# An LSTM product placed ahead of the next column's sums in a fused graph kernel

## The chip, the cores and the metric

The program runs on one core of one Trainium2 chip. The metric is the device time of one execution in microseconds (us). The kernel before was timed three times: 854.16, 857.33 and 858.17 us, so the median is 857.33 us.

## The reference, cut to what matters

Four graph layers are applied one after the other to x (64 graphs, 128 nodes, 128 features). Layer 0 holds the LSTMs that this case is about; layer 3 needs the eigenvectors of a 128x128 Laplacian made from the adjacency matrix, which depend on nothing else in the chain.

```python
# layer 0: two graph convolutions, then for p = 1..4 an LSTM over windows of p nodes
def step(carry, x_t):
    h, c = carry
    g = x_t @ Wih.T + h @ Whh.T + bias
    i, f, gg, o = jnp.split(g, 4, axis=-1)
    c = jax.nn.sigmoid(f) * c + jax.nn.sigmoid(i) * jnp.tanh(gg)
    h = jax.nn.sigmoid(o) * jnp.tanh(c)
    return ((h, c), None)
...
# layer 3
L_norm = d_inv_sqrt[:, None] * L * d_inv_sqrt[None, :]
_, U = jnp.linalg.eigh(L_norm)
agg = jnp.einsum('mn,bnd->bmd', U.T, features)
```

Layers 1 and 2 are a graph attention and a causal self-attention; the change does not touch them.

## The kernel before, in words

The kernel does two things at once from about 20 to 530 us. One is the reduction of the Laplacian A to tridiagonal form, one column per step, in 126 steps (`STEPS`). It is a serial chain of tiny operations: each needs the one before. The other is layer 0, cut into pieces that stand between the operations of that chain, on the same engines, in an order written out by hand. There is no scheduler: each engine runs its own list in order, and semaphores tie the lists together.

A step i of the column chain runs so (names as in the trace):

- The vector engine (DVE) scales the column to `u` (trace: `VI<-XI,col_root,col_signed`), then makes `y` from the product A times column (`VI<-bank,col_root,col_signed`), and `v`, `p` and `w3` from them.
- The tensor engine (PE) multiplies `p` by V (`bank<-VI`; below called K), while DVE makes `xy`. From both DVE makes the next column (`XI<-xy,bank`) and half of the update of A (`A<-bank,VI,A`, written to A1).
- PE turns `w3` around (line 848), and makes the next column's sums (`bank<-XI`). DVE copies them out (`sa<-bank`, function `column_sums`); GpSimd (POOL) takes a power of them (`col_root<-sa,neg_half`, line 463), which the next `u` waits for.
- DVE finishes the update of A (`A<-bank,col_q,A`), then takes three small values from the sums (`column_signs`). PE multiplies the new A by the column (`bank<-XI,A`; below called the matvec), which the next `y` waits for.

The LSTM work is cut into 72 units (one time step of half a batch of windows), which `timetable` places. A unit has 512 columns, or 336 for p = 3. Its gates are made by PE, a piece at a time: one matmul by `wih` and, where there is a state, one by `whh`; a piece is two passes in the trace. `window(w)` puts pieces in three places per step: behind the matvec of step i (w = 3i), behind K (3i+1), and behind the next step's sums, ahead of its matvec (3i+2). `room` allows three pieces at w = 3i where n is 336, and one or two where it is 512. The scalar engine (ACT) turns each gate into `G` by a sigmoid or a tanh (line 633), in the order input, candidate, forget, output (`gates`).

The four products of a unit are DVE's, and `first_mixer(i, place)` puts them at one of four places of a step: place 0 at its start, place 1 behind the A1 update, place 2 behind `col_q`, directly ahead of `column_sums(i + 1)`, and place 3 at the step's end, behind the A update, `column_signs(i + 1)` and the wait for the finished A. A unit with a state (36 of the 72) has input gate times candidate at place 2 (`T<-G`), forget gate times cell state at place 3 of the same step (`T<-G,C`), their sum at place 0 of the next step (`C<-T`), which ACT takes a tanh of, and the state `H` or `HT` at place 1. The sum waits for a semaphore of the forget product (`l_fc`).

Two of the 36 units fall behind the last column: one in step 125, whose next-column work is missing, and one in step 127, where `tridiagonal(3)`, five small operations on the bounds of the spectrum, stands between places 2 and 3.

Of the kernel before, what the change touches and what calls it, by code (L numbers as in the profile page):

```python
# [304 lines left out]
def build(nc, A_, out_d):  # L305
    with ExitStack() as ctx:
# [91 lines left out]
        def half4(t):  # L398
            return t[:, :].rearrange("p (b d) -> p b d", b=GB)

        def by_window(a, x):

            return a.rearrange("p (g w b) -> p g w b", g=x.gb // GB, b=GB)

        def at_place(x, place):

            return HT[:, ds(x.b0 // GB, x.gb // GB), place:place + (x.nw - 1) * x.p + 1:x.p, :]
# [583 lines left out]
        def _(e):  # L991
# [8 lines left out]
            def rows(b):  # L1000
                return e.bn_stats(out=stat[:, b, :], in_=X[:, b, :])  # L1001
# [14 lines left out]
            def stats_1(n):  # L1016

                o = COLUMNS[n]
                variances(n)
                e.reciprocal(out=var[:, o], in_=var[:, o]).then_inc(stats_in, 1)  # L1020

            def stats_2(n):

                o = COLUMNS[n]
                e.wait_ge(rstd_rt, n)
                net(e.reciprocal(out=dm[:, o], in_=rootv[:, o]))
                net(TT(dm[:, o], dm[:, o], var[:, o], ALU.mult))
                net(TT(dm[:, o], dm[:, o], rootv[:, o], ALU.add))
                net(TS(rstd[:, o], dm[:, o], 0.5, None, ALU.mult))
                STT(nbias[:, o], mean[:, o], -0.5, rstd[:, o], ALU.mult, ALU.mult).then_inc(ln_rdy, 1)  # L1030
# [12 lines left out]
            def masks(part):  # L1043

                if part == 0:
                    net(TS(gmask[:, :], adj[:, :], 0.0, NEG, ALU.is_equal, ALU.mult))
                if part == 1:
                    net(TS(cmask[:, :], upper[:, :], NEG, None, ALU.mult))
                if part == 2:
                    net(TT(sq[:, :], ones[:, :], upper[:, :], ALU.subtract))  # L1050
                if part == 3:
                    net(TT(sq[:, :], sq[:, :], adj[:, :], ALU.mult))
                if part == 4:
                    net(TT(cmask[:, :], cmask[:, :], sq[:, :], ALU.add))
                if part == 5:
                    e.wait_ge(bl_in, 32)
                    net(TT(bias[:, :], bl[:, 0, :], bl[:, 1, :], ALU.add))

            def first_mixer(i, place):

                g = i - GRAPH_AT
                j = i - STATS_AT
                if 0 <= j < 8 and place < 3:
                    e.wait_ge(x_in[j // 2], 16)
                    for b in range(8 * j + (0, 4, 6)[place], 8 * j + (4, 6, 8)[place]):
                        r = rows(b)
                    net(r)
                if place == 3:
                    masks(i - MASKS_AT)
                for n, at in enumerate(FINISH_AT):  # L1070
                    if place == 0 and i == at:
                        stats_1(n + 1)
                    if place == 2 * n and i == at + 1:
                        stats_2(n + 1)
                if place == 0 and 0 <= g - 1 < NG:
                    e.wait_ge(a_s1, g)
                    TT(half4(T[(g - 1) % 2][5]), half4(bank[3]), bias0[:, :].unsqueeze(1).to_broadcast([P, GB, P]), ALU.add).then_inc(a_b0, 1)
                if place == 2 and 0 <= g - 2 < NG:
                    e.wait_ge(a_s3, g - 1)
                    TT(half4(T[g % 2][4]), half4(bank[5]), bias1[:, :].unsqueeze(1).to_broadcast([P, GB, P]), ALU.add).then_inc(a_b1, 1)  # L1080
                if place in (2, 3):
                    for x in PRODUCT_AT.get(i, []):
                        u, h, n = x.index, x.h, x.n
                        if place == (2 if x.s else 3):
                            e.wait_ge(l_act, x.k0 + 2)
                            if u >= 2:
                                e.wait_ge(l_h, u - 1)
                            TT((T[h][2] if x.s else C[h])[:, 0:n], G[h][:, 0, 0:n], G[h][:, 2, 0:n], ALU.mult).then_inc(l_ig, 1)
                        if place == 3 and x.s:
                            e.wait_ge(l_act, x.k0 + 3)  # L1090
                            TT(T[h][4][:, 0:n], G[h][:, 1, 0:n], C[h][:, 0:n], ALU.mult).then_inc(l_fc, 1)
                if i in FINISH_UNIT_AT:
                    x = FINISH_UNIT_AT[i]
                    u, h, n = x.index, x.h, x.n
                    if place == 0 and x.s:
                        e.wait_ge(l_fc, x.c)
                        e.wait_ge(l_ig, u + 1)
                        TT(C[h][:, 0:n], T[h][4][:, 0:n], T[h][2][:, 0:n], ALU.add).then_inc(l_c, 1)
                    if place == 1:
                        e.wait_ge(l_t, u + 1)  # L1100
                        o = by_window(H[h][:, 0:n], x) if x.s < x.p - 1 else at_place(x, x.p - 1)
                        TT(o, by_window(G[h][:, 3, 0:n], x), by_window(T[h][3][:, 0:n], x), ALU.mult).then_inc(l_h, 1)
# [144 lines left out]
            signs_done = column_signs(0)  # L1247
            for i in range(STEPS):
                first_mixer(i, 0)
                xi, gam, live, rest = XI[i % 2], GAM[:, 0, i:i + 1], GAM[:, 1, i:i + 1], slice(i + 1, P)  # L1250
                u, v = VI[:, 0, i + 2:i + 3], VI[:, 0, i + 1:i + 2]
# [21 lines left out]
                if i < STEPS - 1:  # L1273
                    e.wait_ge(ch_e, m)
                    STT(XI[(i + 1) % 2][:, 0:2], xy[:, :, 1], bank[1][:, 5:6], xy[:, :, 0], ALU.mult, ALU.subtract).then_inc(x_ready, 1)
                link.note(STT(A1[:, rest], bank[1][:, 6:P + 5 - i], w3, A[:, rest], ALU.mult, ALU.add))
                first_mixer(i, 1)
                link.note(STT(c("q"), w3, bank[1][:, 4:5], p, ALU.mult, ALU.add))
                a = link.n
                first_mixer(i, 2)  # L1280
                if i + 1 < STEPS:
                    column_sums(i + 1)
# [314 lines left out]
```

## Time and profile before

| quantity | value |
|---|---|
| median of three executions | 857.33 us (854.16 to 858.17) |
| the profiled execution | 854.29 us, of which the span from the first to the last instruction is 852.3 us |
| PE busy | 767.2 us (90%) |
| DVE busy | 707.1 us (83%) |
| ACT busy | 497.1 us (58%) |
| POOL busy | 186.4 us (22%) |
| mean granted PE clock | 0.974 |
| column chain with LSTM units that have a state | about 193 to 517 us |

Busy time counts an instruction from its start to its end. On DVE the next instruction can start before the one ahead of it ends, so starts are what tell the pace. "Idle before" in a row is the engine's own gap and what ended it.

### The profile page before, as it was taken

What the parts mean: (1) busy time and instruction counts of PE and PEld (TensorE: products, weight loads), DVE (VectorE), ACT (ScalarE), POOL (GpSimd) and SP (SyncE); (2) the same over time, 40 slices, a digit from 0 to 9 for tenths busy, and PEclk for the clock granted to TensorE, in tenths of its full rate; (3) what the DMA queues carried; (4) which work ended last, traced back from release to release, by engine and by line L of the source; (5) the groups of instructions that cost most, each with busy time, mean ns of one, the idle gap of its engine ahead of it and who ended that gap; (6) DMA issues with size and microseconds to landing.
All of it is one profiled execution on the core that took longest, in us unless ns stands there. A gap on an engine that the chain in (4) does not pass through costs nothing.

```text
span 852.3 us, 13730 instructions
## 1 busy us (share of the span) xinstructions
PE 767.2 (90%) x3738; PEld 508.8 (60%) x3738; DVE 707.1 (83%) x3445; ACT 497.1 (58%) x1115; POOL 186.4 (22%) x387
## 2 busy tenths in 40 slices
PE   4699989999998999999999998769978879797998
PEld 3578854445554566666545554647756656576765
DVE  6898779999887898888877878999989999788533
ACT  0379966664444444444433434458967868698675
POOL 3111112222121221121212211523113423250000
PEclk9999999999999999999999999879999989899999
DMA  9200000000000000000000000000000000000122
GB/s 273 61 3 1 1 1 1 1 1 0 1 1 1 2 1 0 1 2 2 0 1 0 1 1 0 2 0 1 2 1 2 1 1 2 0 1 1 50 75 75
DMA packets 13970, 12.16 MB, mean 14 GB/s; under 512 B 1091, under 2 KB 10822, under 8 KB 13894
## 3 DMA queue, kind: packets, MB, share of 16 engines
q1 hardware_dynamic: 10992, 8.47, 3.4%
q10 hardware_dynamic: 2902, 2.82, 1.1%
q8 instruction: 30, 0.49, 0.3%
q14 instruction: 46, 0.38, 0.2%
HBM read 7.10 MB, written 4.19 MB: 13 GB/s over the span
## 4 chain that ended last, share of the span: by engine, by line
issue 44%; DVE 22%; PE 18%; POOL 11%; ACT 3%; POOLq 0%; DVEq 0%
PE bank L740 17%; POOL col_root L463 7%; POOL XI L467 3%; DVE tt L993 3%; DVE stat L1001 3%; DVE HT L993 2%; DVE X L994 2%; DVE uu L993 2%; ACT T L691 1%; PE bank L750 1%; DVE sm L1142 1%; ACT T L569 1%; DVE wih L993 1%; DVE T L993 1%; DVE sm L1138 1%
## 5 line engine op out<-in xcount | busy, mean ns | idle before, releaser
L633 ACT ACTIVATE G<-bank,bias 128x512 f32<-128x512 f32 (+1 forms) x252 | 158.6, 634 | 181.3 <-PE bank L740 161.8
L740 PE MATMUL bank<-HT,wih 128*128 128x512 f32 (+1 forms) x504 | 246.0, 576 | 0.4 <-ACT HT L619 0.4
L463 POOL TENSOR_TENSOR col_root<-sa,neg_half 128x1 f32<-128x1 f32 x126 | 69.0, 548 | 409.5 <-DVE sa L995 409.5
L740 PE MATMUL bank<-H,whh 128*128 128x512 f32 (+1 forms) x288 | 137.6, 560 | 1.3 <-DVE H L993 0.8
L573 ACT COPY T<-bank 128x512 f32<-128x512 f32 x138 | 80.5, 586 | 56.0 <-PE bank L740 37.6
L569 ACT ACTIVATE T<-X,nbias,rstd 128x128 f32<-128x128 f32 x256 | 104.4, 483 | 6.6 <-DVE nbias L994 6.6
L740 PEld LDWEIGHTS bank<-HT,wih 128*128 128x128 f32 x504 | 81.0, 193 | 16.8 <-issue 10.2
L740 PEld LDWEIGHTS bank<-VI 128*128 128x128 f32 x254 | 45.0, 196 | 76.5 <-DVE VI L993 56.9
L740 PEld LDWEIGHTS bank<-XI,A 128*128 128x128 f32 x252 | 44.6, 196 | 57.3 <-DVE A L994 48.5
L750 PE MATMUL bank<-ident,T 128*128 128x128 f32 x256 | 39.8, 282 | 32.5 <-ACT T L691 25.2
L994 DVE SCALAR_TENSOR_TENSOR XI<-xy,bank 128x2 f32<-128x2 f32 x125 | 28.2, 225 | 43.4 <-PE bank L740 35.3
L740 PE MATMUL bank<-VI 128*128 128x129 f32 (+63 forms) x254 | 49.2, 275 | 15.6 <-DVE VI L993 15.4
L626 ACT ACTIVATE T<-C 128x512 f32<-128x512 f32 (+1 forms) x72 | 41.5, 576 | 33.7 <-DVE C L993 33.4
L740 PEld LDWEIGHTS bank<-XI 128*128 128x128 f32 x252 | 39.5, 198 | 29.0 <-DVE XI L994 15.4
L1001 DVE BATCH_NORM_STATS2 stat<-X 128x6 f32<-128x128 f32 x256 | 55.0, 277 | 0.2
L740 PEld LDWEIGHTS bank<-H,whh 128*128 128x128 f32 x288 | 46.6, 191 | 13.2 <-issue 6.8
L750 PEld LDWEIGHTS bank<-ident,T 128*128 128x128 f32 x256 | 29.5, 143 | 38.4 <-ACT T L691 29.1
L740 PE MATMUL bank<-XI,A 128*128 128x2 f32 x252 | 40.2, 229 | 9.7 <-DVE A L994 9.7
L995 DVE TENSOR_SCALAR VI<-XI,col_root,col_signed 128x1 f32<-128x1 f32 x126 | 33.7, 268 | 13.3 <-POOL col_root L463 12.8
L484 POOL TENSOR_TENSOR G<-M,d 128x512 f32<-128x512 f32 (+2 forms) x20 | 24.5, 1235 | 90.9 <-DVE HT L993 67.5
L994 DVE SCALAR_TENSOR_TENSOR X<-bank,sm,X 128x128 f32<-128x128 f32 x128 | 35.8, 341 | 9.7 <-PE bank L740 9.5
L993 DVE TENSOR_TENSOR tt<-HT,G 128x64 f32<-128x64 f32 (+1 forms) x128 | 39.5, 309 | 3.8
(357 smaller groups left out, 1657.2 us busy)
## 6 DMA issues: line engine op xcount, KB each, us to landing
out_x<-T SPq DMA_DIRECT2D x16, 256.0 KB, 2.2
wih<-in_WihT ACTq DMA_DIRECT2D x1, 1024.0 KB, 12.0
whh<-in_WhhT ACTq DMA_DIRECT2D x1, 1024.0 KB, 17.8
qkvT<-in_WqkvT ACTq DMA_DIRECT2D x1, 192.0 KB
wg<-in_Wg ACTq DMA_DIRECT2D x2, 64.0 KB
l3w<-in_L3W ACTq DMA_DIRECT2D x2, 64.0 KB
adjT<-in_adjT ACTq DMA_DIRECT2D x1, 64.0 KB
adj<-in_adj SPq DMA_DIRECT2D x1, 64.0 KB, 2.0
```

The costliest lines, as they stand in the source:

```text
L463: e.tensor_tensor(out=col["root"][:, :], in0=sa[:, 0:1], in1=neg_half[:, :], op=ALU.pow).then_inc(root_ready, 1)
L467: e.tensor_copy(out=XI[(i + 1) % 2][:, 2:3], in_=ident[:, ds(i + 2, 1)]).then_inc(oh_ready, 1)
L569: i = e.activation(T[g % 2][0][:, ds(b % GB * D, D)], X[:, b, :], ACT.Relu, bias=nbias[:, b:b + 1], scale=rstd[:, b:b + 1])
L573: e.copy(out=dst[:, :], in_=src[:, :]).then_inc(done, 1)
L626: e.activation(T[x.h][3][:, 0:x.n], C[x.h][:, 0:x.n], ACT.Tanh).then_inc(l_t, 1)
L633: e.activation(G[x.h][:, gate, 0:n], gate_bank(k)[:, 0:n], ACT.Tanh if gate == 2 else ACT.Sigmoid, bias=bias[:, 4 * (x.p - 1) + gate:4 * ( ...
L740: mm = lambda out, l, r, start=True, stop=True: e.matmul(out, l, r, start=start, stop=stop)
L750: i = e.transpose(dst[:, ds(b * P, P)], src[:, ds(b * P, P)], ident[:, :])
L993: TT = lambda o, a, b, op: e.tensor_tensor(out=o, in0=a, in1=b, op=op)
L994: STT = lambda o, a, s, b, o0, o1: e.scalar_tensor_tensor(out=o, in0=a, scalar=s, in1=b, op0=o0, op1=o1)
L995: TS = lambda o, a, s1, s2, o0, o1=None: e.tensor_scalar(o, a, s1, s2, o0, *([o1] if o1 else []))
L1001: return e.bn_stats(out=stat[:, b, :], in_=X[:, b, :])
```

## The change: forget gate times cell state moves from place 3 to place 2

```diff
                             TT((T[h][2] if x.s else C[h])[:, 0:n], G[h][:, 0, 0:n], G[h][:, 2, 0:n], ALU.mult).then_inc(l_ig, 1)
-                        if place == 3 and x.s:
+                        if place == 2 and x.s:
                             e.wait_ge(l_act, x.k0 + 3)
                             TT(T[h][4][:, 0:n], G[h][:, 1, 0:n], C[h][:, 0:n], ALU.mult).then_inc(l_fc, 1)
```

No instruction is added or removed, and the lists of PE, ACT, POOL and SyncE are the same in both kernels. DVE's list in step 77, which is one of the 336-wide units' (T12 is the product of input gate and candidate, T14 that of forget gate and cell state):

```order
 L993 TENSOR_TENSOR T12<-G1 128x336
+L993 TENSOR_TENSOR T14<-G1,C1 128x336
 L995 TENSOR_SCALAR sa<-bank0 128x3
 L994 SCALAR_TENSOR_TENSOR A<-bank7,col_q,A1 128x50
@@ -1461,5 +1462,4 @@
 L1242 TENSOR_SCALAR col_size<-sa 128x1
 L995 TENSOR_SCALAR GAM<-sa 128x1
-L993 TENSOR_TENSOR T14<-G1,C1 128x336
 L993 TENSOR_TENSOR C1<-T14,T12 128x336
 L995 TENSOR_SCALAR VI<-XI0,col_root,col_signed 128x1
```

The product now stands ahead of the sums' copy and of the A update, and the sum of the two products follows the small values directly. 34 steps of the column chain have this form, 16 of them 336 wide and 18 of them 512 wide. In step 127, behind the last column, DVE's list changes so (`col_lo` to `col_sgm` are `tridiagonal(3)`):

```order
 L993 TENSOR_TENSOR T12<-G1 128x512
+L993 TENSOR_TENSOR T14<-G1,C1 128x512
 L994 SCALAR_TENSOR_TENSOR col_lo<-col_mxe,col_mnd 128x1
 L994 SCALAR_TENSOR_TENSOR col_w<-col_mxe,col_mxd 128x1
@@ -2346,5 +2347,4 @@
 L995 TENSOR_SCALAR col_w<-col_w 128x1
 L1220 TENSOR_SCALAR col_sgm<-col_w 128x1
-L993 TENSOR_TENSOR T14<-G1,C1 128x512
 L993 TENSOR_TENSOR C1<-T14,T12 128x512
```

Here the five small operations come behind the product and its wait for the forget gate.

## Rows read from the trace of the kernel before

**Rows 1.** Groups of PE weight loads, 290 to 405 us: busy, mean ns | idle before

```profile
L740 PEld LDWEIGHTS bank<-XI,A 128*128 128x128 f32 x62 | 9.5, 188 | 13.4 <-DVE A L994 12.8
```

**Rows 2.** Timeline, DVE in step 77 (336 wide): start us, us, operation

```profile
332.72 0.50 DVE L993 TENSOR_TENSOR T<-G 128x336 f32<-128x336 f32 x1
333.14 0.15 DVE L995 TENSOR_SCALAR sa<-bank 128x3 f32<-128x3 f32 x1
333.21 0.26 DVE L994 SCALAR_TENSOR_TENSOR A<-bank,col_q,A 128x50 f32<-128x50 f32 x1
...
333.57 0.49 DVE L993 TENSOR_TENSOR T<-G,C 128x336 f32<-128x336 f32 x1
334.10 0.51 DVE L993 TENSOR_TENSOR C<-T 128x336 f32<-128x336 f32 x1
334.52 0.27 DVE L995 TENSOR_SCALAR VI<-XI,col_root,col_signed 128x1 f32<-128x1 f32 x1
...
335.91 0.22 DVE L994 SCALAR_TENSOR_TENSOR XI<-xy,bank 128x2 f32<-128x2 f32 x1
```

**Rows 3.** Timeline, PE in the same stretch

```profile
333.52 0.38 PE L740 MATMUL bank<-XI,A 128*128 128x2 f32 x2 [0.19 <-DVE A L994]
333.76 0.81 PE L740 MATMUL bank<-H,whh 128*128 128x336 f32 x2
...
334.98 0.73 PE L740 MATMUL bank<-H,whh 128*128 128x336 f32 x2
335.54 0.32 PE L740 MATMUL bank<-VI 128*128 128x51 f32 x2
```

**Rows 4.** Timeline, A update and matvec of step 76 (336 wide)

```profile
329.13 0.26 DVE L994 SCALAR_TENSOR_TENSOR A<-bank,col_q,A 128x51 f32<-128x51 f32 x1
...
329.52 0.32 PE L740 MATMUL bank<-XI,A 128*128 128x2 f32 x2
```

**Rows 5.** Timeline, step 78: sums' copy, and the next u behind POOL

```profile
336.78 0.15 DVE L995 TENSOR_SCALAR sa<-bank 128x3 f32<-128x3 f32 x1
...
337.70 0.27 DVE L995 TENSOR_SCALAR VI<-XI,col_root,col_signed 128x1 f32<-128x1 f32 x1 [0.35 <-POOL col_root L463]
```

**Rows 6.** Timeline, step 100 (512 wide, two pieces behind the matvec)

```profile
419.45 0.25 DVE L994 SCALAR_TENSOR_TENSOR A<-bank,col_q,A 128x27 f32<-128x27 f32 x1
...
420.13 0.28 PE L740 MATMUL bank<-XI,A 128*128 128x2 f32 x2
...
422.07 0.30 PE L740 MATMUL bank<-VI 128*128 128x28 f32 x2
...
422.51 0.23 DVE L994 SCALAR_TENSOR_TENSOR XI<-xy,bank 128x2 f32<-128x2 f32 x1
```

**Rows 7.** Timeline, step 109 (512 wide, one piece behind the matvec)

```profile
454.84 0.69 ACT L633 ACTIVATE G<-bank,bias 128x512 f32<-128x512 f32 x1 [1.25 <-PE bank L740]
...
455.40 0.69 DVE L993 TENSOR_TENSOR T<-G 128x512 f32<-128x512 f32 x1
...
455.83 0.28 PE L740 MATMUL bank<-XI 128*128 128x3 f32 x2
...
456.15 0.16 DVE L995 TENSOR_SCALAR sa<-bank 128x3 f32<-128x3 f32 x1
...
456.92 0.28 PE L740 MATMUL bank<-XI,A 128*128 128x2 f32 x2
...
457.89 0.27 DVE L995 TENSOR_SCALAR VI<-XI,col_root,col_signed 128x1 f32<-128x1 f32 x1
...
458.66 0.40 PE L740 MATMUL bank<-VI 128*128 128x19 f32 x2 [0.50 <-DVE VI L993]
```

**Rows 8.** Timeline, step 127, behind the last column

```profile
526.06 0.15 DVE L994 SCALAR_TENSOR_TENSOR col_lo<-col_mxe,col_mnd 128x1 f32<-128x1 f32 x1
...
526.82 0.15 DVE L1220 TENSOR_SCALAR col_sgm<-col_w 128x1 uint32<-128x1 uint32 x1
527.18 0.69 DVE L993 TENSOR_TENSOR T<-G,C 128x512 f32<-128x512 f32 x1 [0.21 <-ACT G L633]
```

**Rows 9.** Windows: us, busy (count) of PE, PEld, DVE, ACT, POOL; PE clock, DMA share, GB/s

```profile
263.70:267.10 3.40, 1.85 (x8) 1.24 (x9) 3.22 (x16) 0.63 (x1) 0.23 (x2) 1.00 0.00 0
267.10:270.50 3.40, 3.40 (x6) 1.46 (x6) 1.62 (x12) 1.21 (x2) 0.64 (x2) 0.50 0.00 0
```

## The prediction, written before the result was known

> **What bounds the kernel now.** I read the timeline of the column steps first, DVE's rows beside PE's, then the groups of idle time on PE's weight loads, and last the windows with the granted clock. The reader is to see that two engines take turns in bounding a step. In a step with a forget product DVE runs without a gap from the candidate product to the next `u` [rows 2]. At the same time PE waits: the matvec of step 77 starts at 333.52 us, 0.31 behind the start of the A update at 333.21, with the weight load's wait for A ended by it [rows 2, 3]. Over the 336-wide stretch this wait sums to 12.8 us [rows 1]. Behind the matvec stand three LSTM pieces, and directly behind the last of them K: its second half starts one pass (0.28 us, half of the 0.57 between the starts of the last piece and K, 334.98 to 335.54) ahead of K, so K starts the moment PE is free [rows 3]. The next column XI starts at 335.91, which is 0.37 behind K's start [rows 2, 3]; it also stands 1.39 behind `u` (334.52), which is DVE's own shortest way. Both roads arrive together. So the A update is not a side road here: A, matvec, three pieces, K, XI is a chain without slack, and the old place of the product, behind the A update, kept that chain short.
>
> **What the change moves, part by part.** Nothing is added; 36 products move. Two are behind the last column, 34 in the chain, in three kinds by what PE has behind the matvec. I counted them in the timetable's windows and PE's timeline.
>
> *What the product costs in its new place.* The 336-wide product T<-G at 332.72 holds the next instruction until 333.14, so 0.42 us; the 512-wide one holds it 0.60 where nothing is waited for (in step 109 `sa` comes 0.75 behind it, since it waits for the sums that PE started at 455.83, 0.32 earlier [rows 7]; the 0.60 is the 0.69 of the row less the overlap of 0.08 that the 336 one shows, 0.50 against 0.42 [rows 2, 7]). `sa`, the A update and everything behind them come later by that.
>
> *What it gives in its old place.* From the old product's start to the sum's start is 0.53 in step 77 (333.57 to 334.10), because the sum waits for the product's end. That falls out, so DVE reaches `u` 0.53 - 0.42 = 0.11 earlier. But the next `u` also waits for POOL's power: in step 78 it starts 0.92 behind `sa` [rows 5]. In step 77 `sa` moves to 333.56, the power lets `u` go at 334.48, against 334.52 before. The gain is 0.04.
>
> *Kind 1, 16 steps, 336 wide (three pieces behind the matvec; in the last, two of 512).* Eight are like step 77: A waits 0.42 longer, the matvec starts at 333.94, three pieces and K follow in the same 2.02 us (333.52 to 335.54), K starts at 335.96 and XI at 336.33: 0.42 later, 0.40 by finer reading over the eight. Eight are like step 76: there the matvec at 329.52 is 0.39 behind A's start at 329.13 and not 0.31, since PE came from an earlier piece, so 0.08 is slack and 0.34 passes [rows 4]; over the eight I read 0.33. One step (69) has 0.2 of slack at K. Sum: 8 x 0.40 + 8 x 0.33 - 0.2 = 5.6 us lost.
>
> *Kind 2, 8 steps, 512 wide, two pieces (once three of 336) behind.* In step 100 the A update at 419.45 would let the matvec go at about 419.76 (0.31 behind it), but it starts at 420.13, since a 512-wide piece is ahead of it on PE. Of the 0.60, 0.37 is slack, and 0.23 reaches K at 422.07. XI at 422.51 is 0.44 behind K and needs 0.34 to 0.37, so another 0.1 is slack, and 0.13 passes [rows 6]. The others lie between 0.09 and 0.18; together 1.1 us. PE is then later by 0.1 to 0.2 than DVE, and in about half of these steps the next `sa` sits on PE's sums: 0.6 more. Sum 1.7 us lost.
>
> *Kind 3, 10 steps, 512 wide, one piece or none behind.* In step 109 `sa` waits for PE's sums until 456.15, and the product fills that wait: the new `sa` comes at 455.40 + 1.20 = 456.60, 0.45 later and not 0.60. The way from there to `u` loses the old product with its wait (0.72). So `u` comes 0.27 earlier. K had waited 0.50 for DVE, which covers the later matvec, so the 0.27 is kept [rows 7]. Six to seven steps are like this, three have 0.18. Sum 2.5 us gained.
>
> *The two behind the last column.* In step 125 the product fills a short wait of the A update: 0.1 gained. In step 127 the product starts at 527.18 when the forget gate comes, and the five small operations from 526.06 to 526.97 that had used the wait now stand behind it [rows 8]: up to 0.9 lost, of which later waits for PE may swallow a third. I take 0.6; net 0.5 lost.
>
> *The added wait.* The forget gate must be there earlier. Its latest arrival in the chain is step 109, ACT's row from 454.84 to 455.53, while the product would start at 456.00 [rows 7]. It costs nothing; if ACT were 0.5 later, `sa` and all behind it on DVE would wait.
>
> Sum: 5.6 + 1.7 - 2.5 + 0.5 = 5.3 us lost. The profiled execution took 854.29 us (span 852.3, so 2.0 around it); this gives 859.6. That execution was 3.0 under the median of 857.33; from the median the sum gives 862.6. I take the middle, 861.0.
>
> **A rule weighed against the rows.** Rows 2 show the next DVE instruction starting 0.08 us ahead of the end of a 336-wide product. The Trainium skill, "VectorE: DVE Perf Modes", section "The DRAIN you can't avoid", says that the next op does not start until the pipe is empty, and that leaving out a semaphore wait between two ops saves nothing. It speaks against this change: nothing of kind 3's gain from the dropped wait would be left, and the A update would be later by the whole duration. The row disagrees with it by 0.08 per product, so I keep it as a rival only.
>
> **The rivals.**
>
> *DVE alone counts (faster).* If the matvec had slack after all, for example if K could go ahead of the pieces, each step would be worth its change of `u`: 16 x 0.06 + 8 x 0.13 + 10 x 0.25 = 4.5 us gained, 852.8 us from the median. For it: DVE shows no gap in rows 2. Against: K starts as PE's last pass ends [rows 3]. It decides if the matvec's delay is under the slack at K, which is 0 in kind 1.
>
> *Products hold DVE for their whole duration (slower, more).* 0.50 instead of 0.42 in 16 steps adds 1.3, 0.69 instead of 0.60 adds 0.7 in kind 2 and takes 0.9 from kind 3: 8.2 us lost, 865.5 us.
>
> *The granted clock falls once or twice more.* In this trace the clock was at half (1.2 GHz) from 267.1 to 270.5, behind a stretch of 3.4 us in which PE was busy for only 1.85; PE was then busy for all 3.40, so a fall costs about 1.7 us [rows 9]. The change adds 0.3 to 0.4 us of idle PE in front of many matvecs. Two more falls: 5.3 + 3.4 = 8.7 lost, 866.0 us. Against: single gaps stay under 1 us, and the pieces fill the rest.
>
> *The lateness is made good.* If pieces behind a late matvec ran closer together, or the neighbouring step's slack took most of kind 1's delay, the losses of kinds 1 and 2 would halve to 3.7, and with kind 3 and the end the sum is 1.7 lost: 859.0 us. For it: step 69's slack. Against: steps 71 to 73, 76 to 78 and so on follow one another with K at the 1.02 behind `u` of rows 2 and 3 (334.52 to 335.54), which is the tight value.
>
> **How the numbers follow.** 0.5% is 4.3 us, about what a measurement of this kernel can tell from no change. Forecast 0.66 (its 5.3 is near that bound: 0.40 above, 0.26 under); DVE alone 0.12 (0.09 faster, 0.03 same); whole durations 0.07, slower; clock 0.08 (0.07 slower, 0.01 same); made good 0.07 (0.06 same, 0.01 faster). Faster 0.10, same 0.36, slower 0.54. The forecast's own range is 858 to 864; with the rivals I leave out most of "DVE alone" below 855 and little above 866.5.
>
> **What would show it.** Kind 1: the weight load of `XI,A` waits about 0.4 longer per step (the 12.8 us become about 18), XI waits for K by 0.4 more in the steps behind them, and steps 76 to 78 grow. Kind 3: steps like 109 shrink by about 0.27 us. The wait of `C<-T` goes. Wrong if the matvec wait grows and XI does not move, or if the forget gate shows up as what DVE waits for inside the chain.

## The result, and the profile after

The changed kernel takes 861.46 us in the median of 15 executions (856.99 to 863.15); the kernel before, executed 15 times beside it and earlier, 855.15 us (851.37 to 858.17). The ratio is 1.0063, with a 95% interval of 1.0048 to 1.0078, which is 5.4 us lost (4.1 to 6.7). Forecast were 861.0 us and 5.3 us lost. The time of 861.0 was taken halfway between two sums from three executions; with the median of all 15 the forecast loss gives 860.5.

| quantity, profiled execution | before | after |
|---|---|---|
| span | 852.3 us | 858.7 us |
| mean granted PE clock | 0.974 | 0.972 |
| DVE busy | 707.1 us | 703.4 us |
| idle before XI, all steps, behind PE | 35.3 us | 47.6 us |
| idle before the matvec's weight load, behind A, all steps | 48.5 us | 63.3 us |

One thing differs from what was said ahead of the prediction. DVE's list is shorter by one semaphore wait per moved product: the trace of the kernel before has 766 such records on DVE, that of the change 730. They took no time of their own (between the last of the small values and the next product it is 0.06 us with and without one), but they shift the numbering of DVE's instructions, which matters further down.

The groups of PE's weight loads in the same 31 steps as in [rows 1] (now 290 to 412 us; busy, mean ns | idle before):

```profile
L740 PEld LDWEIGHTS bank<-XI,A 128*128 128x128 f32 x62 | 9.5, 188 | 19.4 <-DVE A L994 18.8
```

The wait for A has grown from 12.8 to 18.8 us. The timeline of step 77, DVE, answers to [rows 2]:

```profile
334.58 0.50 DVE L993 TENSOR_TENSOR T<-G 128x336 f32<-128x336 f32 x1
335.00 0.50 DVE L993 TENSOR_TENSOR T<-G,C 128x336 f32<-128x336 f32 x1
335.42 0.15 DVE L995 TENSOR_SCALAR sa<-bank 128x3 f32<-128x3 f32 x1
335.49 0.26 DVE L994 SCALAR_TENSOR_TENSOR A<-bank,col_q,A 128x50 f32<-128x50 f32 x1
...
335.85 0.50 DVE L993 TENSOR_TENSOR C<-T 128x336 f32<-128x336 f32 x1
336.31 0.27 DVE L995 TENSOR_SCALAR VI<-XI,col_root,col_signed 128x1 f32<-128x1 f32 x1
...
338.18 0.23 DVE L994 SCALAR_TENSOR_TENSOR XI<-xy,bank 128x2 f32<-128x2 f32 x1 [0.59 <-PE bank L740]
```

and PE in the same step to [rows 3]:

```profile
335.80 0.38 PE L740 MATMUL bank<-XI,A 128*128 128x2 f32 x2 [0.60 <-DVE A L994]
336.05 0.81 PE L740 MATMUL bank<-H,whh 128*128 128x336 f32 x2
...
337.82 0.32 PE L740 MATMUL bank<-VI 128*128 128x51 f32 x2
```

From T<-G to the matvec it was 0.80 us (332.72 to 333.52) and is 1.22 (334.58 to 335.80). From the matvec to K it is 2.02 as before, and XI is 0.36 behind K. XI now waits 0.59 for PE, 1.87 behind `u` and not 1.39, though DVE reached `u` 0.07 sooner behind T<-G (1.73 against 1.80).

The time from one XI to the next, step by step, after less before, shows where the whole change lies. The sums over the kinds, in us (kinds 1 to 3 are those of the prediction):

| kind | steps | forecast | measured |
|---|---|---|---|
| 1: 336 wide | 16 | +5.6 | +5.5 |
| 2: 512 wide, two or three pieces behind the matvec | 8 | +1.7 with the steps behind them | +1.9, and +0.6 in the steps behind them (step 117 left out) |
| 3: 512 wide, one piece or none | 10 | -2.5 | -2.4 |
| behind the last column: XI of step 124 to the table M | 2 | +0.5 | +0.8 (19.05 to 19.82) |

The rows add up to 6.4 us here, near the upper end of what the timing gives. The span has grown by 6.4 too, but by chance: outside the rows of the table gains and losses cancel. Steps 5 and 6 are 1.3 us shorter (DVE waits less for PE there), step 22 is 1.5 shorter (a clock fall that is missing), steps 60 and 61 are 1.6 longer, and there are short gaps of DVE of both signs, of which the next section tells. Step 117 is left out of the steps behind kind 2, since it is 0.28 shorter by such a gap in the profile before. Steps 60 and 61 have a longer clock fall, at the place of [rows 9] (columns as there):

```profile
260.90:264.30 3.40, 1.78 (x9) 1.10 (x9) 3.23 (x13) 0.63 (x1) 0.61 (x2) 0.99 0.00 0
264.30:271.10 6.80, 6.67 (x12) 3.37 (x12) 2.42 (x18) 1.89 (x3) 0.69 (x2) 0.50 0.00 0
```

It lasts 6.8 us and not 3.4, behind the same two steps without pieces on PE. But a fall that the kernel before had at 120.4 us is missing here. And two of the experiments below, "mixed" and "mixed, both products of kind 1 behind A", have the same lists up to step 68, and one shows this fall with 3.4 us (from 265.3), the other with 6.8 (from 260.9). So its length belongs to the single execution. Over all executions the clock is the same: the mean is 0.973 in the 15 of the change, and 0.972 to 0.974 in the kernel before on the four chips of the experiments.

### The profile page after: what moved, and what is told of

Read it like the earlier page. It is cut to its first block, busy times and chain, and to the rows that moved or that the text cites. A ratio compares the mean times of both kernels' runs of the same rounds, so it can differ in the third digit from the quotient of the medians.

```text
span 858.7 us, 13687 instructions
## 1 busy us (share of the span) xinstructions
PE 770.0 (90%) x3731; PEld 507.4 (59%) x3738; DVE 703.4 (82%) x3445; ACT 500.0 (58%) x1115; POOL 185.8 (22%) x387
## 3 DMA queue, kind: packets, MB, share of 16 engines
HBM read 7.10 MB, written 4.19 MB: 13 GB/s over the span
## 4 chain that ended last, share of the span: by engine, by line
issue 45%; DVE 22%; PE 18%; POOL 11%; ACT 3%; POOLq 0%; DVEq 0%
PE bank L740 17%; POOL col_root L463 7%; POOL XI L467 3%; DVE tt L993 3%; DVE stat L1001 3%; DVE HT L993 2%; DVE X L994 2%; DVE uu L993 2%; ACT T L691 1%; PE bank L750 1%; DVE sm L1142 1%; DVE wih L993 1%; DVE T L993 1%; ACT T L569 1%; DVE sm L1138 0%
## 5 line engine op out<-in xcount | busy, mean ns | idle before, releaser
L740 PEld LDWEIGHTS bank<-XI,A 128*128 128x128 f32 x252 | 42.9, 195 | 69.9 <-DVE A L994 63.3
L994 DVE SCALAR_TENSOR_TENSOR XI<-xy,bank 128x2 f32<-128x2 f32 x125 | 28.1, 225 | 53.2 <-PE bank L740 47.6
L740 PE MATMUL bank<-XI,A 128*128 128x2 f32 x252 | 42.5, 238 | 14.7 <-DVE A L994 12.0
```

The source lines that it names most:

```text
L740: mm = lambda out, l, r, start=True, stop=True: e.matmul(out, l, r, start=start, stop=stop)
L994: STT = lambda o, a, s, b, o0, o1: e.scalar_tensor_tensor(out=o, in0=a, scalar=s, in1=b, op0=o0, op1=o1)
```

## The experiments

All keep PE's, ACT's and POOL's lists and move DVE's products only, unless it is said otherwise. The product's place is chosen by the unit's kind (1 to 3 as above, 4 behind the last column):

```diff
-                        if place == 3 and x.s:
-                            e.wait_ge(l_act, x.k0 + 3)
-                            TT(T[h][4][:, 0:n], G[h][:, 1, 0:n], C[h][:, 0:n], ALU.mult).then_inc(l_fc, 1)
+                        if x.s and place == FC_AT[kind(x)]:
+                            forget(x)
```

With `{1: 3, 2: 3, 3: 3, 4: 3}` it is the kernel before, with four times 2 the change. The line numbers of the kernels below differ from those before by the added lines. Two more places are used: "sums", behind `column_sums(i + 1)`, and "A", behind the A update and ahead of `column_signs(i + 1)`. Per kernel: the median, the ratio to the kernel before on the same chip with its 95% interval, and the sums of XI-to-XI changes by kind in its profile, in us:

| kernel | median us | ratio (interval) | kind 1 | kind 2 | kind 3 |
|---|---|---|---|---|---|
| the change | 861.46 | 1.0063 (1.0048 to 1.0078) | +5.5 | +1.9 | -2.4 |
| kind 1 alone | 860.4 | 1.0044 (1.0026 to 1.0061) | +5.6 | +0.1 | -0.2 |
| kind 2 alone | 856.43 | 1.0004 (0.9988 to 1.0021) | -0.6 | +1.9 | -0.2 |
| kind 3 alone | 852.05 | 0.9960 (0.9941 to 0.9979) | -0.4 | +0.5 | -2.7 |
| kind 4 alone | 858.16 | 1.0015 (0.9997 to 1.0033) | 0.0 | 0.0 | 0.0 |
| kind 1 behind the sums | 859.49 | 1.0047 (1.0026 to 1.0068) | +5.6 | +0.1 | -0.2 |
| kinds 1 to 3 behind A | 851.36 | 0.9955 (0.9935 to 0.9974) | -0.5 | -0.9 | -1.1 |
| mixed | 852.0 | 0.9972 (0.9951 to 0.9993) | -0.5 | -0.9 | -2.4 |
| one piece left out, old order | 854.4 | 0.9990 (0.9974 to 1.0007) | 0.0 | 0.0 | 0.0 |
| one piece left out, kind 1 moved | 854.01 | 0.9989 (0.9975 to 1.0003) | 0.0 | +0.1 | -0.2 |
| mixed, both products of kind 1 behind A | 854.17 | 0.9977 (0.9960 to 0.9994) | +1.5 | -0.9 | -2.4 |

Where a kernel changed nothing in a kind, its sum still comes out between -0.6 and +0.5. This is not noise of the single execution. DVE has short gaps with no wait to explain them; three rows show one:

```profile
382.53 0.27 DVE L995 TENSOR_SCALAR VI<-XI,col_root,col_signed 128x1 f32<-128x1 f32 x1 [0.27 <-issue]
382.90 0.27 DVE L1008 TENSOR_SCALAR VI<-XI,col_root,col_signed 128x1 f32<-128x1 f32 x1 [0.27 <-issue]
379.85 0.27 DVE L1012 TENSOR_SCALAR VI<-XI,col_root,col_signed 128x1 f32<-128x1 f32 x1 [0.27 <-issue]
```

They are step 90 in the kernel before, in kind 4 alone and in one piece left out in the old order. These three have the same DVE list up to step 124, and the same seven gaps, in steps 47, 69, 80, 90, 95, 112 and 117, of 0.15 to 0.37 us. Over all twelve profiles, from 190 to 517 us, 59 instructions that waited for no other engine start over 0.1 us later behind the one ahead of them than the same pair does at its closest. With DVE's records (semaphore waits included) numbered from 0, 56 of the 59 have a number that leaves 63 when divided by 128, and the other three leave 64. So the gaps go by the place in DVE's list. An order that drops semaphore waits shifts all later instructions against them: the change has gaps in steps 75, 80, 107 and 119 instead. What happens at every 128th record no run here shows.

For a sum this means: each kernel carries its own pattern of gaps, each worth up to 0.35 us. Kind 1 in the change comes out 0.8 us low by it, since the kernel before had gaps in steps 69, 80 and 95 that cost it time (0.19, 0.25 and 0.35) and the change has none there that costs any. Half a us is the size of this effect in the other sums.

**Kind 1 alone.** `FC_AT = {1: 2, 2: 3, 3: 3, 4: 3}`

> Only the 16 products of the 336-wide units stand at place 2 (three pieces behind the matvec); the other 20 stay at place 3. Theory (the A update, the matvec, the three pieces, K and XI are a chain without slack, so each product ahead of the A update passes on what it is longer than the matvec's slack): 5.6 us slower than before, about +0.65%, and the matvec's weight load waits about 6 us more in that stretch. Rival (DVE alone counts): 1 us faster. Rival (the lateness is made good by half): 2.8 us slower, +0.33%.

Its 16 products cost 5.6 us in the profile and 3.8 us (2.2 to 5.2) in the timing. The matvec's weight loads wait for A as in the change:

```profile
L753 PEld LDWEIGHTS bank<-XI,A 128*128 128x128 f32 x62 | 9.5, 188 | 19.2 <-DVE A L1007 18.6
```

Six us more wait, and a time well away from "faster". The timing's interval holds the lower rival's 2.8 and ends just short of the theory's 5.6; the steps decide between them: thirteen of the sixteen are longer by 0.36 to 0.42 us each, and the other three (69, 80, 95) are those in which the kernel before has a gap.

**Kind 2 alone.** `{1: 3, 2: 2, 3: 3, 4: 3}`

> Only the 8 products of 512-wide units with two pieces (once three) behind the matvec stand at place 2. Theory: 1.7 to 2.0 us slower, +0.2%. Rival (DVE alone counts): 1.0 us faster, -0.1%.

+1.9 in the steps themselves (each of the eight longer by 0.18 to 0.28), but a timing from -1.0 to +1.8 us does not tell it from nothing. The profile is against the rival, the timing cannot decide.

**Kind 3 alone.** `{1: 3, 2: 3, 3: 2, 4: 3}`

> Only the 10 products of 512-wide units with at most one piece behind the matvec stand at place 2. Theory: the product fills DVE's wait for the next column's sums and the dropped wait of the sum of products is won too: 2.4 us faster, -0.3%. Rival (a product holds DVE for its whole duration, nothing won from the dropped wait): 0.9 us less, 1.5 us faster. Rival (any product ahead of the A update delays): slower.

2.7 us gained by steps, 3.4 (1.8 to 5.1) in the timing. Step 109, DVE, against [rows 7]:

```profile
455.07 0.68 DVE L1006 TENSOR_TENSOR T<-G 128x512 f32<-128x512 f32 x1
455.67 0.68 DVE L1006 TENSOR_TENSOR T<-G,C 128x512 f32<-128x512 f32 x1
456.27 0.15 DVE L1008 TENSOR_SCALAR sa<-bank 128x3 f32<-128x3 f32 x1
...
456.67 0.68 DVE L1006 TENSOR_TENSOR C<-T 128x512 f32<-128x512 f32 x1
```

Each product holds DVE for 0.60 and not for its 0.68, and the sum follows the small values with no wait. A product ahead of the A update is therefore not bad by itself.

**Kind 4 alone.** `{1: 3, 2: 3, 3: 3, 4: 2}`

> Only the two products behind the last column (steps 125 and 127) stand at place 2. Theory: 0.5 to 0.8 us slower, within the noise of the timing; in the profile the way from XI of step 124 to the table M grows from 19.0 us to about 19.8. Rival (later waits for PE swallow it): no change of that way.

The way from XI of step 124 to M is 19.60 us against 19.05. DVE in step 127, against [rows 8]:

```profile
527.29 0.69 DVE L1006 TENSOR_TENSOR T<-G,C 128x512 f32<-128x512 f32 x1 [0.97 <-ACT G L646]
527.90 0.15 DVE L1007 SCALAR_TENSOR_TENSOR col_lo<-col_mxe,col_mnd 128x1 f32<-128x1 f32 x1
...
528.85 0.69 DVE L1006 TENSOR_TENSOR C<-T 128x512 f32<-128x512 f32 x1
```

DVE's wait for the forget gate is 0.97 where it was 0.21, with the five small operations behind it. Up to there step 125 had gained 0.22, and step 127 loses 0.77. The cost is seen in the profile; the timing's interval reaches no change.

**Kind 1 behind the sums.** `{1: "sums", 2: 3, 3: 3, 4: 3}`

> The 16 products of the 336-wide units stand between the copy of the sums (sa) and the A update; all others stay at place 3. So POOL's power starts on time, but the A update is as late as in the change. Theory (the A update's lateness is what costs): 5 to 6 us slower, as with all 16 at place 2. Rival (the late sums and the power behind them cost): no slower than before, 1 to 2 us faster.

DVE, POOL and PE in step 77:

```profile
331.86 0.50 DVE L1006 TENSOR_TENSOR T<-G 128x336 f32<-128x336 f32 x1
332.28 0.15 DVE L1008 TENSOR_SCALAR sa<-bank 128x3 f32<-128x3 f32 x1
332.35 0.49 DVE L1006 TENSOR_TENSOR T<-G,C 128x336 f32<-128x336 f32 x1
332.52 0.74 POOL L476 TENSOR_TENSOR col_root<-sa,neg_half 128x1 f32<-128x1 f32 x1 [3.32 <-DVE sa L1008]
332.77 0.26 DVE L1007 SCALAR_TENSOR_TENSOR A<-bank,col_q,A 128x50 f32<-128x50 f32 x1
...
333.08 0.38 PE L753 MATMUL bank<-XI,A 128*128 128x2 f32 x2 [0.60 <-DVE A L1007]
```

`sa` is on time, 0.42 behind T<-G as before, and A and the matvec are as late as in the change. The cost is the same: +5.6 by steps, ratio 1.0047 against 1.0044. So the late sums and the power behind them are not the cause in kind 1; the late A update is.

**Kinds 1 to 3 behind the A update.** `{1: "A", 2: "A", 3: "A", 4: 3}`

> All 34 products of the column chain stand directly behind the A update, ahead of the three small values; the two behind the last column stay at place 3. Sums and A update are on time, and the small values cover the wait of the sum of products for the forget product. Theory: u comes 0.1 us earlier in each; in the 16 336-wide steps K has no slack, so nothing is won there; in the 18 others it is: 2 us faster, -0.25%. Rival (DVE alone counts): 34 x 0.11 = 3.7 us faster, -0.4%. Rival (a product holds DVE for its whole duration): no change.

Step 77:

```profile
332.37 0.26 DVE L1007 SCALAR_TENSOR_TENSOR A<-bank,col_q,A 128x50 f32<-128x50 f32 x1
...
332.55 0.50 DVE L1006 TENSOR_TENSOR T<-G,C 128x336 f32<-128x336 f32 x1
332.68 0.38 PE L753 MATMUL bank<-XI,A 128*128 128x2 f32 x2 [0.18 <-DVE A L1007]
...
333.56 0.27 DVE L1008 TENSOR_SCALAR VI<-XI,col_root,col_signed 128x1 f32<-128x1 f32 x1
...
335.06 0.22 DVE L1007 SCALAR_TENSOR_TENSOR XI<-xy,bank 128x2 f32<-128x2 f32 x1 [0.21 <-PE bank L753]
```

`u` comes 0.12 sooner behind the A update (1.19 against 1.31), and XI then waits 0.21 for PE: where K is tight the gain turns into that wait. In kind 3 the 0.12 is kept (step 109: 4.31 to 4.19 us from XI to XI). In kind 2 it is kept up to step 64 and 0.05 to 0.09 are left in steps 100, 116 and 118; some of the steps behind kind 2 (49, 50, 63, 101) are 0.04 to 0.10 longer, as they are in the change. By steps 2.5 us are gained, 0.5 of them in kind 1; that half us is mostly gaps again (69 and 95 shorter, 85 longer), while the other thirteen steps change by 0.03 or less. The timing gives 3.8 us (2.2 to 5.6), so by time alone the rival with 3.7 us could stand; the steps rule it out.

**Mixed.** `{1: "A", 2: "A", 3: 2, 4: 3}`

> The 10 products of 512-wide units with at most one piece behind the matvec stand at place 2, the 24 others of the chain directly behind the A update, the two behind the last column at place 3. Theory: 2.4 us from the ten and 0.9 us from the eight 512-wide ones: 3.3 us faster than before, -0.4%, 9 us faster than the change. Rival (the gains are noise): no change.

By steps 3.8 us gained, by time 2.4 (0.6 to 4.2). It beats both the kernel before and the change. It is 1.3 us better by steps than the order with all behind A, but their intervals overlap and the medians (852.0 and 851.36) stand the other way, so which of the two is the faster stays open.

**One piece behind the matvec left out, in the old order and with kind 1 moved.** In the 16 windows that follow a kind 1 product (a `wih` piece is cut to 16 columns in the same way):

```diff
+            NARROW = {[y for y in PIECES_AT[3 * x.pool_at + 3] if y[2] or not y[0].s][-1][:3] + (3 * x.pool_at + 3,) for x in UNITS if kind(x) == 1}
...
+                        m = 16 if (x, q, state, w) in NARROW else n
+                        t = mm(o[:, 0:m], whh[:, x.p - 1, gate, :], H[h][:, 0:m], start=False)
```

> The order of before, but in the 16 windows behind the matvec that follow a 336-wide forget product, one piece (one gate's recurrent part, once a gate of a first step) is computed on 16 columns only: this work is left out. Theory: DVE and PE both are tight there, so taking 0.5 us of PE work out of each gains little: 0 to 1 us faster. Rival (PE alone bounds these steps): 16 x 0.5 = 8 us faster.

> As thin_before (one piece behind the matvec left out in the same 16 windows), with the 16 products of the 336-wide units at place 2. Theory: the 0.5 us taken out of the chain from the matvec to K now covers the late A update, so the 16 products cost nothing: within 1 us of thin_before, -1 to 0, against 5.6 us with all pieces there. Rival (late sums or DVE's order cost by themselves): 5 us slower than thin_before.

Half a us of PE's work out of each of 16 steps gains 0.9 us in the timing (0.6 lost to 2.2 gained) and nothing in the kinds' sums: the rival's 8 us are excluded. With that room, the 16 moved products cost next to nothing: ratios 0.9990 and 0.9989, and 0.0 us in kind 1 where it was +5.6. In twelve of the steps they still cost 0.02 to 0.08, against 0.36 to 0.42 with all pieces there; the gaps of steps 69, 80 and 95 in the kernel before bring the sum to zero. Step 77 of the second, PE and DVE:

```profile
334.06 0.38 PE L753 MATMUL bank<-XI,A 128*128 128x2 f32 x2 [0.60 <-DVE A L1011]
...
335.52 0.29 PE L753 MATMUL bank<-H,whh 128*128 128x16 f32 x2
335.66 0.40 PE L753 MATMUL bank<-VI 128*128 128x51 f32 x2
...
336.10 0.23 DVE L1011 SCALAR_TENSOR_TENSOR XI<-xy,bank 128x2 f32<-128x2 f32 x1 [0.24 <-PE bank L753]
```

The matvec waits 0.60 for A as in the change, but K follows 1.60 behind it and not 2.02. So it is the pieces between the matvec and K that make the late A update cost.

**Both products of kind 1 behind the A update.** As mixed, and in kind 1 also `T<-G` at "A":

```diff
+                        if kind(x) == 1:
+                            e.wait_ge(l_act, x.k0 + 2)
+                            e.wait_ge(l_h, x.index - 1)
+                            TT(T[x.h][2][:, 0:x.n], G[x.h][:, 0, 0:x.n], G[x.h][:, 2, 0:x.n], ALU.mult).then_inc(l_ig, 1)
```

> As the mixed order (ten products at place 2, the 24 others behind the A update), and in the 16 336-wide steps the product of input gate and candidate stands behind the A update too. So the A update comes 0.42 us earlier there than in the kernel before. Theory (K and DVE's way to u were both tight): in the eight steps in which the matvec waited for A (like 77) K comes earlier and the 0.11 us that DVE has won counts now; in the eight others (like 76) PE itself holds the matvec and nothing changes: 0.9 us more than mixed, 4.2 us faster than before. Rival (the A update alone bounds these steps): 16 x 0.4 = 6 us more than mixed, 9.7 us faster than before.

This one came out otherwise. The steps like 77 gained 0.05 each and not 0.11; the steps like 76, where nothing was to change, lost about 0.3 each. Kind 1 is 2.0 us worse than in mixed. Step 76:

```profile
326.02 0.23 DVE L1007 SCALAR_TENSOR_TENSOR XI<-xy,bank 128x2 f32<-128x2 f32 x1 [0.85 <-PE bank L753]
...
326.87 0.16 DVE L1008 TENSOR_SCALAR sa<-bank 128x3 f32<-128x3 f32 x1 [0.32 <-PE bank L753]
326.95 0.27 DVE L1007 SCALAR_TENSOR_TENSOR A<-bank,col_q,A 128x51 f32<-128x51 f32 x1
...
327.14 0.52 DVE L1006 TENSOR_TENSOR T<-G 128x336 f32<-128x336 f32 x1
```

XI is late there and `sa` must wait for PE's sums. The candidate product, in its old place, had filled that wait; taken out, DVE idles 0.32 and carries the product behind it. I had looked at K and the matvec only and had not asked what the product covered. The rival (6 us more than mixed) is excluded by the steps and by the timing, 2.0 us (0.5 to 3.4) faster than before and not 9.7.

## Why the prediction was right

- *The chain without slack, and kind 1.* 5.6 forecast, 5.5 measured. Two experiments carry the mechanism: with the sums on time and only A late the cost stays, and with room between matvec and K it goes. That the amount fits so closely is luck. Steps like 76 were put at 0.33 and measured 0.36 to 0.42: the matvec waits for A now, and from there to K it is 2.02 us (331.33 to 333.35 in the trace after), a little more than where the matvec follows a piece. Against that stand two gaps of DVE that the kernel before had, in steps 80 and 95, and that the forecast left in (0.6 together). The slack of 0.2 at K in step 69, which it did take off, is a third gap of this sort (0.19, ahead of `T<-G,C`); in kind 2 alone and kind 3 alone, which leave step 69 as it was, it is gone. Without the three gaps the sixteen products cost 6.3 us.
- *Kind 2.* Mis-sized: the steps themselves were put at 1.1 and measured 1.9. Each was put at about 0.14, and those like 42, 44 and 48 measured 0.27. Of the 2.04 us from matvec to K in step 100 of the trace after, 0.10 is new (1.94 in [rows 6]): the matvec takes 0.38 and not 0.28. The knock-on to the steps behind was put at 0.6 and is 0.6 without step 117; but with all products behind A the steps 49, 50, 63 and 101 are longer by the same 0.04 to 0.10, though kind 2 itself is faster there, so it is not shown that the lateness is what they pay for. With it kind 2 lost about 2.4, against 1.7.
- *Kind 3.* 2.5 forecast, 2.4 and 2.7 measured. The parts given for it (six or seven steps of 0.27, three of 0.18) add up to 2.2 to 2.4 and not to 2.5. Measured were 0.18 to 0.20 in three steps and 0.28 to 0.32 in five; steps 107 and 112 have gaps.
- *Behind the last column.* 0.5 forecast, 0.55 in kind 4 alone, but from two errors: step 125 gained 0.22 (0.1 forecast) and step 127 lost 0.77 (0.6), since nothing swallowed its lateness. The 0.8 of the change is this and a gap of 0.22 at T<-G of step 125.
- *The forget gate's arrival* cost nothing in the chain: no DVE wait for ACT is there before step 127.
- *The rivals.* "DVE alone counts" is excluded by kind 1 alone and by the order behind A, in which 0.12 per step turns into a wait for K. "Products hold DVE for their whole duration" is excluded by starts 0.42 and 0.60 apart in the rows above, under durations of 0.50 and 0.68. "The clock falls more often" is not seen: the mean clock of the executions is 0.973 on both sides, and the longer fall is one execution's. "The lateness is made good" is excluded by about +0.40 in step after step (71, 72, 76, 77, 79 and so on), other than in steps 69 (+0.22), 80 (+0.16) and 95 (+0.01), in which the kernel before has a gap.
- *The rule weighed.* The prediction set the rows against the Trainium skill, "VectorE: DVE Perf Modes", section "The DRAIN you can't avoid". It left out that the same section goes on to say that a next op that is not held starts earlier. The rows (starts 0.42 apart under 0.50, 0.60 under 0.68) agree with that sentence, so they do not go against the section in this. They do go against its other point, that a semaphore between two ops costs nothing: the sum started 0.53 (336 wide) and 0.72 (512 wide) behind a product that it waited for, where an instruction that did not wait started 0.42 and 0.60 behind.

By steps the sum is 6.4, 1.1 above the forecast of 5.3, most of it kind 2 and the end. That the timing (5.4, from 4.1 to 6.7) lies nearer to the forecast than to the steps is luck too: its interval holds both.

## What to carry to other kernels

Ask of each place in a list not how long it is but which engine is late next there: the same product at the same place cost 0.4 us where its delay ran into a queue of pieces on the tensor engine, and gained 0.3 where the vector engine had been waiting for the tensor engine anyway. Before an operation is moved away, look at what wait it had covered, and before it is moved ahead, how much slack there is at the next point where two engines' roads meet. A short order change is best judged step by step, from one such point to the next: thirteen of sixteen like steps agreed within 0.06 us where fifteen executions of the whole left an uncertainty of more than one. Steps that fall out of line are to be looked at singly and not averaged in: here they held gaps that belong to the place in the engine's list, and that move when an instruction, or only a semaphore wait, is taken out ahead of them.

## What the runs showed of the hardware that was not expected

- A two-pass matvec on PE takes 0.28 us where its weights were loaded well ahead (step 100 before: load at 419.75, matvec at 420.13) and 0.38 where the load had waited for A and came with it, even though PE was hardly idle. Step 100 after:

```profile
425.90 0.30 PEld L740 LDWEIGHTS bank<-XI,A 128*128 128x128 f32 x2 [0.86 <-DVE A L994]
425.91 0.38 PE L740 MATMUL bank<-XI,A 128*128 128x2 f32 x2
```

- POOL's power of one column takes 0.55 us in the kernel before (547 to 549 ns in 32 steps). In step 77 before, `T<-G,C` starts 0.20 behind it (333.37 and 333.57) and it takes 0.55. It took 0.74 in step 77 with a DVE product started 0.17 ahead of it (kind 1 behind the sums), and up to 0.93 in the orders with the product behind A. In step 77 of that order it began 0.02 ahead of the product:

```profile
332.53 0.92 POOL L476 TENSOR_TENSOR col_root<-sa,neg_half 128x1 f32<-128x1 f32 x1 [2.90 <-DVE sa L1008]
```

  A DVE product that starts at about the same time seems to hold POOL up. It cost nothing, since `u` was waiting for DVE there; no run tested it by itself.
- DVE has gaps of 0.15 to 0.4 us that go by the place in its list: in twelve profiles all 59 of them stand at every 128th record (number 63 or 64 after whole multiples of 128), and kernels with the same DVE list have the same ones. Not every such place shows one; what happens there stays open.
